# An LSTM stage with its batch on the partitions, in a kernel of merged stages on one core

## The reference

```
step(h, c, x_t):  z = x_t @ Wx + b + h @ Wh          # 32 x 512: four gates i, f, o, g
                  c = sigmoid(f) * c + sigmoid(i) * tanh(g)
                  h = sigmoid(o) * tanh(c)

y = LSTM(x, h0=cond, weights of layer 1)             # 128 steps
logits = y @ Wr + br; the two best of 16 experts, weights by softmax over these two
e-th expert: gelu(layernorm(y @ W1[e] + b1[e]) * g1 + be1) @ W2[e] + b2[e]
x = x + sum of the two chosen experts                # all 16 are computed, and weighted
a = LSTM(x, h0=cond, weights of layer 2)             # 128 steps
```

## Time and profile before

| | us |
|---|---|
| median of 3 runs | 4672.22 (4669.35 to 4680.54) |
| profiled execution, its own time | 4662.41 |
| its span in the profile | 4660.6 |
| TensorE busy | 4309.6 (92%) |
| VectorE, ScalarE, GpSimd busy | 2494.8, 1859.3, 761.1 |
| mean granted clock of TensorE | 0.959 |

### The profile page before, as it was taken

The page is one execution under the profiler, slowest core; times in us unless marked ns, Lnnn a source line. Parts: engine busy times, 40 slices in busy tenths (PEclk is TensorE's granted clock), DMA queues, the critical chain, the costliest instruction groups (busy, mean ns, idle before and its releaser), DMA issues. The chain is left out here.

```text
span 4660.6 us, 118083 instructions
## 1 busy us (share of the span) xinstructions
PE 4309.6 (92%) x41087; PEld 3214.5 (69%) x41087; DVE 2494.8 (54%) x7506; ACT 1859.3 (40%) x4669; POOL 761.1 (16%) x3314
## 2 busy tenths in 40 slices
PE   6999999999998999998799999999997887889998
PEld 4556777777876888886355787787875555566666
DVE  5775664555554777776555444666666563421111
ACT  4433443333331444444233222666664452333333
POOL 1111220000001555554122000111111210000000
PEclk9999999999998999998699998999998997989999
DMA  1000000000000000000000000000000100000000
GB/s 53 0 0 25 0 0 25 0 0 0 0 0 10 1 2 1 1 1 1 33 1 0 3 0 0 3 3 3 3 3 2 52 0 1 0 1 0 0 0 18
DMA packets 3080, 28.73 MB, mean 6 GB/s; under 512 B 320, under 2 KB 832, under 8 KB 1216
## 3 DMA queue, kind: packets, MB, share of 16 engines
q1 hardware_dynamic: 2768, 24.81, 1.4%
HBM read 22.71 MB, written 2.10 MB: 5 GB/s over the span
## 5 line engine op out<-in xcount | busy, mean ns | idle before, releaser
L2231 DVE SCALAR_TENSOR_TENSOR experts_acc<-banks,experts_gate,experts_acc 128x128 f32<-128x128 f32 x512 | 144.2, 345 | 461.7 <-PE banks L2177 460.6
L2177 PEld LDWEIGHTS banks<-weights,experts_hidden 128*128 128x128 f32 x2560 | 303.3, 192 | 55.0 <-issue 49.7
L604 DVE TENSOR_REDUCE cells_row_max<-banks 128x4 f32<-128x512 f32 x384 | 238.5, 684 | 161.6 <-PE banks L397 161.6
L2177 PE MATMUL banks<-weights,experts_hidden 128*128 128x128 f32 x2560 | 305.2, 275 | 0.0
L761 PE MATMUL banks<-clock_fill 128*128 128x512 bf16 x932 | 284.8, 394 | 7.4 <-DVE wave_bias_parts L1612 7.4
L2450 ACT ACTIVATE experts_hidden<-banks,weights 128x512 f32<-128x512 f32 x256 | 175.8, 687 | 268.5 <-PE banks L2447 265.2
L1412 PEld LDWEIGHTS banks<-act_a,weights 128*128 128x128 f32 x2032 | 256.1, 196 | 25.6 <-DVE act_a L1670 18.0
L2447 PE MATMUL banks<-act_a,weights 128*128 (+1 forms) x512 | 262.3, 643 | 0.7 <-ACT experts_hidden L2450 0.3
L1412 PE MATMUL banks<-act_a,weights 128*128 (+1 forms) x2032 | 248.7, 281 | 10.8 <-DVE act_a L1670 10.7
L541 ACT ACTIVATE cells_probs<-banks 128x512 f32<-128x512 f32 x384 | 198.2, 603 | 95.0 <-PE banks L437 90.0
L604 DVE TENSOR_REDUCE attn_row_max<-banks 128x4 f32<-128x512 f32 x256 | 159.0, 684 | 134.8 <-PE banks L397 134.8
(11 more groups left out here) (522 smaller groups left out, 9904.5 us busy)
## 6 DMA issues: line engine op xcount, KB each, us to landing
weights<-in_p SPq DMA_DIRECT2D x1, 2894.5 KB, 17.2
weights<-in_p SPq DMA_DIRECT2D x1, 2894.0 KB, 9.2
weights<-in_p SPq DMA_DIRECT2D x2, 1364.0 KB, 7.1
x_res<-in_x SPq DMA_DIRECT2D x1, 2048.0 KB, 14.9
out_x<-x_res SPq DMA_DIRECT2D x1, 2048.0 KB, 6.3
weights<-in_p SPq DMA_DIRECT2D x1, 1836.0 KB, 10.9
weights<-in_p SPq DMA_DIRECT2D x1, 1835.5 KB, 6.9
weights<-in_p SPq DMA_DIRECT2D x1, 1344.5 KB, 9.8
```

The costliest lines, as they stand in the source:

```text
L604: dve.tensor_reduce(mt[:, 4 * g:4 * g + 4], bank, AX_X, ALU.max).then_inc(s["max_ready"], 1)
L2177: last = pe.matmul(ps[:, 2 + e % 2, t * P:(t + 1) * P], hs[lo:lo + n, (tile + f) % slots, t * P:(t + 1) * P], out_rhs(e, f, lo, n), start= ...
L2231: last = dve.scalar_tensor_tensor(out=acc[:, t, :], in0=ps[:, 2 + e % 2, t * P:(t + 1) * P], scalar=g[:, t, e:e + 1], in1=acc[:, t, :], op ...
```

## The change

Batches go to the partitions. The state (128 features x 32 batches) is now the loaded operand and the weights stream: a gate block is a product of 256 columns (four gates x one half of the features) that comes out on 32 partitions. The 128 output partitions are half 0 of recurrence 0, half 0 of recurrence 1, half 1 of recurrence 0, half 1 of recurrence 1. So 4 products make what 8 made, and cell, gates and tanh run on 128 partitions x 64 for both recurrences at once. The input products take the same form, made one step ahead, from quads of inputs that GpSimd copies next to each other.

The new state is batch by feature, and the next step needs it feature by batch. So VectorE writes it in two half-height products into a block-diagonal tile `hb`, TensorE multiplies this with a constant that picks and turns (`turned`, 128 x 64 out), ScalarE copies the result into a ring of 16 positions (`state`), and `h_ready` now comes from there. GpSimd copies the later recurrence's ring into `a` in quads, and the earlier one's into the experts' source. The logits read the ring directly.

The banks are dealt anew: two for gates (two steps each), one for the turned state, one of its own (`SIDE`) for logits, turned gates and totals, two for hidden products, one for the turned units, one for the expert outputs. The calls in each engine's `body` are reordered, the routing of VectorE is cut into single operations (at most six per step) between the others, and the Gelus of an item run in the step of its turn, two before the state's copy and two behind it. The variance is summed halved, which drops one GpSimd operation of 13.

```diff
...
-    HBANK, TURN, OUT = 4, 6, 7
-    RSRC, HSRC, GSRC = 4, 16, 20
-    NEWTON, ROUTING = 12, 15
-    FOLD, FOLD_BIAS = (0, 2, 4, 5), 7
+    STATE, SIDE, HBANK, TURN, OUT = 2, 3, 4, 6, 7
+    HSRC, GSRC, KEPT = 14, 20, WAVE_LAG + AHEAD + 3
+    NEWTON, ROUTING = 11, 16
+    FOLD, FOLD_BIAS = (3, 7, 4, 5), 3
+    HALF = P // 2
...
+        th = sb("gates_tanh", [P, 4, HALF])
+        og, c2, fc, ic, tc = (sb(n, [P, HALF]) for n in ("output_gate", "c_twice", "fc", "ic", "tc"))
+        hb = sb("state_by_batch", [P, P])
+        ring = sb("states", [P, 2, WAVE_PERIOD, NB])
+        xq = sb("inputs", [P, 2, 2, AHEAD * NB])
...
+            def input_quad(j, time, parity):
+                xs = positions(core.x, time, AHEAD)
+                pool.tensor_tensor(xq[:, j, parity, :].rearrange("p (t b) -> p t b", t=AHEAD), xs,
+                                   unit_quad, ALU.mult).then_inc(s["x_earlier" if j else "x_later"], 1)
...
+            def keep(time, m):
+                states = ring[:, 0, 4 * m:4 * m + 4, :]
+                pool.tensor_tensor(positions(core.a, time, AHEAD), states, unit_quad, ALU.mult).then_inc(s["kept"], 1)
...
-            def pre(st, known):
-                k, quad = st.c % 4, st.c // 4 + 1
-                for j in range(2):
...
-                    out = ps[:, bank, k * AHEAD * NB:(k + 1) * AHEAD * NB].rearrange("p (t b) -> p t b", t=AHEAD)
-                    pe.matmul(out, packs[j]("Wx", k * P, P), positions(core.x, time_of(st, j, 4 - k), AHEAD),
-                              start=False, stop=False, skip_group_check=True)
...
+            def bias(st, known):
...
+                pe.matmul(ps[:, (st.c + 1) % 2, :], pick[0:68, :], bias_w[0:68, int(early), :].unsqueeze(
+                    1).broadcast_to([68, 2, 4 * HALF]), start=True, stop=False, skip_group_check=True)
+
+            def gates_part(st, j, half, state, name):
+                lo, at = NB * (2 * half + j), st.c // 2 % 2 * 4 * HALF
+                return pe.matmul(ps[lo:lo + NB, st.c % 2, at:at + 4 * HALF].rearrange(
+                    "p (g f) -> p g f", g=4), state, half_of(packs[j], name, half), start=False,
+                    stop=name == "Wh", skip_group_check=True)
...
+                for half in range(2):
+                    for j in js:
+                        gates_part(st, j, half, xq[:, j, parity, k * NB:(k + 1) * NB], "Wx")
...
             def recurrent(st, known):
-                k, bank = st.c % 4, 2 * (st.c // 4 % 2)
                 past(pe, s["h_ready"], st.s())
-                for j in running(st, known):
-                    first = known and st.c == WAVE_LAG * (1 - j)
-                    state = const("cond").unsqueeze(1) if first else positions(core.a, time_of(st, j, -1))
-                    for z in range(4):
-                        lo = (z * AHEAD + k) * NB
-                        last = pe.matmul(ps[:, bank + j, lo:lo + NB].unsqueeze(1), packs[j]("Wh", z * P, P), state,
-                                         start=False, stop=True, skip_group_check=True)
+                for half in range(2):
+                    for j in running(st, known):
+                        first = known and st.c == WAVE_LAG * (1 - j)
+                        state = const("cond") if first else ring[:, j, (st.c - 1) % WAVE_PERIOD, :]
+                        last = gates_part(st, j, half, state, "Wh")
                 last.then_inc(s["z_done"], 1)
+
+            def turned(st):
+                pe.wait_ge(s["batch_ready"], st.s(1))
+                pe.matmul(ps[:, STATE, 0:2 * NB], hb[:, :], const("half_pick"), start=True, stop=True).then_inc(
+                    s["turned_ready"], 1)
...
             def body(st, known):
                 recurrent(st, known)
+                it = item(st, HID, known)
+                if it is not None:
+                    hidden(st, *it)
+                later = Wave(st.i, st.c + 1)
+                if later.c % 4 < 2:
+                    bias(st, known)
+                if later.c < P + WAVE_LAG:
+                    inputs(later, known)
                 if known:
                     fold(st)
                     fill_ends(st)
-                summed = tile_at(st, TOTAL, known)
-                if summed is not None:
-                    total(st, summed)
-                scored, turned = tile_at(st, LOGITS, known), tile_at(st, GTURN, known)
-                if scored is not None:
-                    logits(st, scored)
-                if turned is not None:
-                    gates_turn(st, turned)
-                it = item(st, HID, known)
+                tile = tile_at(st, LOGITS, known)
+                if tile is not None:
+                    logits(st, tile)
+                tile = tile_at(st, GTURN, known)
+                if tile is not None:
+                    gates_turn(st, tile)
+                it = item(st, TURNED, known)
                 if it is not None:
-                    hidden(st, *it)
+                    turn(it[0], it[2])
+                tile = tile_at(st, TOTAL, known)
+                if tile is not None:
+                    total(st, tile)
                 it = item(st, OUTPUT, known)
                 if it is not None:
-                    output(it[0], it[2], summed)
-                it = item(st, TURNED, known)
-                if it is not None:
-                    turn(it[0], it[2], scored, turned)
-                pre(st, known)
+                    output(it[0], it[2])
+                turned(st)
...
-                act.activation(tc[:, lo:hi, :], c2[:, lo:hi, :], ACT.Tanh, scale=0.5).then_inc(s["tc_ready"], 1)
+                act.activation(tc[:, :], c2[:, :], ACT.Tanh, scale=0.5).then_inc(s["tc_ready"], 1)
+
+            def state(st, known):
+                if st.c % 4 == 0:
+                    if not known or WAVE_PERIOD <= st.c < P + WAVE_PERIOD:
+                        act.wait_ge(s["source_ready"], st.every4(WAVE_PERIOD) + 1)
+                    if not known or WAVE_LAG + WAVE_PERIOD <= st.c:
+                        act.wait_ge(s["kept"], st.every4(WAVE_LAG + WAVE_PERIOD) + 1)
+                act.wait_ge(s["turned_ready"], st.s(1))
+                act.activation(ring[:, :, st.c % WAVE_PERIOD, :], ps[:, STATE, 0:2 * NB].rearrange(
+                    "p (j b) -> p j b", j=2), ACT.Copy).then_inc(s["h_ready"], 1)
...
+                gate_tanh(st)
+                cell_tanh(st)
                 group = group_at(st, 2, known)
                 if group is not None:
                     distance(group)
-                it = item(st, OUTPUT, known)
+                it = item(st, HID, known)
                 if it is not None:
-                    gelus(it[0], it[2])
-                gate_tanh(st, lo, hi)
+                    square(it[0], it[2])
                 tile = tile_at(st, GTURN, known)
                 if tile is not None:
                     gates_kept(st, tile)
-                cell_tanh(st, lo, hi)
-                it = item(st, HID, known)
-                if it is not None:
-                    square(it[0], it[2])
+                turned = item(st, TURNED, known)
+                if turned is not None:
+                    gelus(turned[0], turned[2], 0)
+                state(st, known)
+                if turned is not None:
+                    gelus(turned[0], turned[2], 1)
...
-            def state(st, lo, hi):
+                dve.scalar_tensor_tensor(out=c2[:, :], in0=fc[:, :], scalar=0.5, in1=ic[:, :], op0=ALU.mult,
+                                         op1=ALU.add).then_inc(s["c_ready"], 1)
+                dve.tensor_scalar(og[:, :], th[:, 2, :], 0.5, 0.5, ALU.mult, ALU.add).then_inc(s["gate_ready"], 1)
+
+            def state(st):
                 dve.wait_ge(s["gate_ready"], st.s(1))
                 dve.wait_ge(s["tc_ready"], st.s(1))
-                out = core.a[:, :].rearrange("p (b t) -> p t b", t=P)[
-                    :, bass.ds(time_of(st, lo), hi - lo, WAVE_LAG), :]
-                dve.tensor_tensor(out, tc[:, lo:hi, :], og[:, lo:hi, :], ALU.mult).then_inc(s["h_ready"], 1)
+                for half in range(2):
+                    rows = slice(half * HALF, (half + 1) * HALF)
+                    last = dve.tensor_tensor(hb[rows, rows], tc[rows, :], og[rows, :], ALU.mult)
+                last.then_inc(s["batch_ready"], 1)
...
-                js = running(st, known)
-                lo, hi = js[0], js[-1] + 1
-                for part_, route in enumerate((route_first, route_second, route_gates)):
-                    group = group_at(st, part_, known)
-                    if group is not None:
-                        route(group)
-                cell(st, lo, hi)
+                route(st, known, 0)
+                cell(st)
+                route(st, known, 1)
                 tile = tile_at(st, LOGITS, known)
                 if tile is not None:
                     logits(tile)
+                state(st)
+                route(st, known, 2)
```

(20 more changed lines are left out.)

325 lines of the change are left out of this document (179 added, 146 removed).

## The result

The changed kernel takes 4593.2 us (median of 4 runs, 4591.3 to 4595.6) beside 4673.1 us for the one before (4 runs, 4669.4 to 4680.5): ratio 0.983, 95% interval 0.981 to 0.984, a gain of 80 us. The prediction said 4637 us, a gain of 35: the right sign, and less than half of the size.

The account below looks back on a forecast made before the run. TensorE's queue was taken as the bound: 126 middle steps from 5.53 to 5.04 us give -61.7, ends and prologue +27, together -34.7 us. From the profiled 4662.4 this is 4627.7, as a median 4637; range 4588 to 4698.

Parts of the forecast that it names:

- The queue sum: TensorE's products in a plain middle step, added start to start: 4.99 us before, 4.40 us after the change.
- The round trip: Each step's end: turning the state back, ScalarE's copy and the way to the next recurrence, 0.9 us (bounds 0.7 and 1.2).
- the drain rival: TensorE waits out a 0.16 us tail at each of three tiling switches per step: +0.26, 4670 us, no change; chance 0.10.
- the 0.15 of the earlier trace for a pair: Two switches around a strip block between full-width neighbours cost 0.15 us together, read from the attention's context products.
- I keep the 0.54 whole: 4.94: Middle step's 0.54 us beyond plain products (once-in-four rows, loop's jump, waits) stays unchanged, making 4.94 us.
- 0.10 for the clock: Middle steps: idle array once per step brings one clock fall in 15 steps, adding 0.10 us for 5.04 us.
- the first rival: Middle steps gain more: 0.25 us less from spread routing and separate bank, clock stays up: 4.69 a step, 4593; chance 0.18.
- The prologue: Stage start: drops about 1.5 us, first inputs taking 0.6 for 1.9.
- The ends: Quiet steps at both ends: 3.6 us against 2.59, costing +18 in the first 21 steps and +10 in the last ten.
- The wait for units: Hidden products behind the recurrence: 0.4 us of wait for VectorE's units, hidden in the steady run by TensorE's late queue.
- The copy's place behind two Gelus: ScalarE's state copy: costs nothing, as two Gelus end before the state is turned; otherwise up to 0.8 us late.
- the 0.2%: Whole kernel: median 4672.2 us lies 0.2% above the profiled 4662.4; the same shift takes 4627.7 to 4637.5.

Follow-up runs that it names:

- run 7: Changed kernel with the hidden products put back behind the inputs, logits and turned gates, VectorE's new order kept: 4567.1 us.
- run 5: Changed kernel with two parts of the routing (twelve of seventeen operations) put back as blocks of six ahead of the cell: 4606.8 us.
- run 12: Changed kernel with the total back in the expert outputs' bank and VectorE's store of the residual ahead of the state: 4624.2 us.
- run 2: Kernel before with only VectorE's calls reordered (variance, guess and units ahead of the weighted sums), old layout and TensorE order: 4628.5 us.
- run 6: Changed kernel with ScalarE's copy of the turned state behind all four Gelus of the step instead of behind two: 4606.5 us.
- run 10: Changed kernel with the total back in the expert outputs' bank, VectorE's store of the residual staying behind variance and units: 4676.9 us.
- Run 1: Kernel before with only its 28 filler products moved ahead of TensorE's two waits at the stage's start: 4659.2 us beside 4667.2.
- run 9: Kernel before, unchanged, profiled once more: 4672.6 us.
- run 8: Changed kernel with hidden products back behind the inputs and VectorE in the old order: 4661.4 us, ratio 0.9982 against the kernel before.
- run 3: Changed kernel with VectorE's calls in the old order (store and weighted sums, units, then variance and guess): 4689.6 us.

## Why the prediction missed

**The queue sum came out right, by two errors that cancel.** TensorE's plain step was put at 4.40 us and is 4.35 to 4.41. The round trip is 0.65 to 0.71 us instead of 0.90. Against it, three changes of form that no wait hides cost 0.14 (recurrence), 0.10 (hidden), 0.14 (inputs) and 0.06 (turn) over the bare 0.43, 0.86, 0.43 and 0.43: 0.44, where the sum held 0.22. So the drain rival's 0.16 for each change was right (0.145 by run 7), and the 0.15 of the earlier trace rows for a pair was too little; the 4670 it gave needed a round trip of 0.9 as well. The Trainium skill, "TensorEngine Tiling (Array Packing)", section "Tiling Modes", says that a change of tiling mode drains TensorE. The trace agrees in so far as each change costs time; what TensorE does in it, no run here shows.

**The failed step: "I keep the 0.54 whole: 4.94. Then 0.10 for the clock".** These two terms carry over all that the middle of before held besides its plain queue, as if the new orders took none of it away, and add falls of the clock to it. The steps of the middle are also not alike, which the prediction took them to be. Both recurrences run only in 96 of the 126 (us, from the starts of the tanhs):

| steps | before, each | after, each | forecast gain | measured gain |
|---|---|---|---|---|
| 32 to 127, both recurrences | 5.54 | 4.92 | 47 | 60 |
| 21 to 31 and 128 to 146, one recurrence | 5.50 | 4.65 | 15 | 26 |

In the 96 steps the 0.10 for the clock is 9.6 us of the 13 that are missing: two falls lie there before and one after, so none were added. Without it the sum gives 4.94, and the full middle takes 4.934. That is luck too, since what the surplus holds has changed. Before, one step in sixteen took 7.05 us for 5.82 with the routing as a block in it, the step at the jump 6.54 for 5.56, and the output products waited 6.9 us of the 80 steps for the residual's store. After, the routing's step takes 5.21 like its neighbours of that kind, and no product waits for the store; instead the hidden products wait 13.6 us for units. So the first rival had its reasons right (routing spread: 13.6 us, run 5; separate bank: 31 us, run 12; no added falls). That it also gave the measured 4593 is luck in the sizes.

In the 30 steps the queue sum itself is wrong. With one recurrence the blocks of before are half as long, but a strip block is not (two strips take the time of four). TensorE's recurrent rows of one such step and the next, before and then after:

```profile
2119.02 1.00 PE L1412 MATMUL banks<-act_a,weights 128*128 128x32 f32 x8
...
2122.68 1.00 PE L1412 MATMUL banks<-act_a,weights 128*128 128x32 f32 x8
```

```profile
2073.30 0.63 PE L1420 MATMUL banks<-weights,wave_states 128*32 128x256 f32 x4 [0.40 <-ACT wave_states L1607]
...
2077.62 0.63 PE L1420 MATMUL banks<-weights,wave_states 128*32 128x256 f32 x4 [0.31 <-ACT wave_states L1607]
```

The plain step grows from 3.66 to 4.32 us where the prediction has it shrink by 0.59. These steps gained all the same: before, they held 27 us of TensorE's waits and 30 us at the 1.2 GHz level, after 12 (mostly the new round trip) and none. Run 2 shows what takes them away: VectorE's new order alone, in the old layout, brings the 30 steps from 165.0 to 144.1 us, and the whole change to 139.4. This order is what the prediction put at nothing when it kept the surplus whole. The two errors here have opposite signs, and only that keeps the miss of the middle at 23.7 us (85.4 - 61.7).

**What a fall costs.** The 0.10 came from the earlier trace rows, read as what an idle piece in every step does. The trace of before has 9 falls: 7 in steps 21 to 30 and 132 to 141, and two in the full middle, both right behind the loop's jump. One of the latter, as a stretch (columns as in the earlier trace rows):

```profile
1719.60:1723.00 3.40, 3.40 (x11) 2.28 (x12) 1.65 (x9) 1.18 (x3) 1.95 (x10) 0.53 0.00 0
```

Ahead of it TensorE had waited 0.74 us for the state (VectorE had stood still for 2.94 us over the jump):

```profile
1717.72 2.09 PE L1412 MATMUL banks<-act_a,weights 128*128 x16 [0.74 <-DVE act_a L1670]
...
1720.43 1.92 PE L1464 MATMUL banks<-wave_w_centred,wave_src 128*128 128x512 f32 x2
```

The step that holds most of it took 6.74 us, the same step of an undisturbed round 5.20: a fall costs 1.54 us. The changed kernel has one fall (from 1859.3, again behind the jump, behind waits of 0.45 and 0.99 us), in a step of 7.21 us for 5.36. At 1.54 us the seven falls of the 30 steps would be 11 us; that is an estimate, since the price was not measured there, and how their gain divides between clock and waits stays open. The count of falls goes with TensorE's longer waits: 0.31 to 0.6 us in every step leaves one or none (changed kernel, run 6), waits of about 2 us every fourth step come with 10 (run 10), waits of up to 0.7 us there with none (run 12). Which waits do it stays open too: one of 0.90 us in step 77 of before brought none.

**The prologue** was put at -1.5 us and gave -9.4. The diff moves the two waits behind the fillers; the prediction priced only the first input products. Run 1 measures the move at -8.1 us.

**The ends** cost 20.9 us for 28 forecast: 3.36 us a quiet step instead of 3.6, from the round trip (0.75 in place of 0.92) and the cell (1.01 in place of 1.13), less 0.07 more for the two half products. The recurrence up to the tanh takes the 0.68 that the prediction gave it.

**The wait for units is not hidden.** The prediction let the queue's lateness cover it; the hidden products wait in 33 of the 81 steps of 1600 to 2000 us, 13.7 us in all. Together with the two changes of form that their new place adds to every second step this costs 26 us (run 7). The copy's place behind two Gelus was rightly priced at nothing: TensorE idles 0.31 to 0.37 us for the copy there, and 0.31 in the quiet step without Gelus. Behind four it costs 13 us (run 6).

**Profiled execution and median.** The forecast carried over the 0.2% by which the median before lies above its profile. The median after lies 0.4 us above its own. Before varies over 11 us from run to run, after over 4; run 9 suggests that falls make a good part of this, and more falls than the first profile has would then be part of the gain of 80 against the profile's 69.6.

**Order, banks and layout need each other.** The prediction gave its whole gain to TensorE's shorter blocks. Layout, banks, spread routing and the early fillers alone give 8 us (run 8), which is what the fillers give by themselves; VectorE's order alone 36 (run 2), both with hidden products in the old place 103 (run 7): 59 more than the sum. With the old order the shorter queue only waits (run 3, run 8); with the old layout the order only helps where TensorE has slack. The new place of the hidden products takes 26 back. And the separate bank, worth 31 by itself, exists only because the gates now fill two banks instead of four.

## What to carry to other kernels

A queue sum of the bounding engine can be right to 1% and the forecast still wrong, because the time around it (waits, clock) changes too: list the waits and every stretch at the lower clock, see what stands ahead of each, and ask whether the change takes it away. Before multiplying a step's sum by a count, ask in which steps it holds: 30 of the 126 here ran one recurrence, and their queue grew. Price an order and a layout together; each alone was worth less than half here. When blocks of one form are split by another, count the changes of form, and look whether a block can fill the gap of a round trip: that was worth 29 to 37 us more.
